# Two stages laid into one block, and the weights of two later stages prepared in the lead-in of the first

## The reference

```python
x = x + attention0(layernorm(x), c, c)   # heads of 8, softmax over 256 columns
x = x + ffn0(layernorm(x))               # of each sequence only the 32 tokens of highest score
x = x + gated_attention1(layernorm(x), c)
x = x + ffn1(layernorm(x))               # weights rounded to -1, 0, 1
x = x + softmax_attention2(layernorm(x), c)  # four square matrices Wq, Wk, Wv, Wo
x = x + gated_ffn2(x) ; ...              # and a last layer
```

## Time and profile before

| | us |
|---|---|
| runs | 1898.48, 1903.65, 1902.52 (median 1902.52) |
| profiled execution | 1898.31 (span 1896.4, mean granted TensorE clock 0.831) |
| first attention, last matmul | 450.4 |
| selected feed-forward, first matmul | 484.8 |
| block of the normed feed-forward's weights | 916.8 to 939.8 |
| block of the softmax attention's weights | 1204.8 to 1216.0 |

### The profile page before, as it was taken

The page is one execution under the profiler, slowest core; times in us unless marked ns, Lnnn a source line. Parts: engine busy times, 40 slices in busy tenths (PEclk is TensorE's granted clock), DMA queues, the critical chain, the costliest instruction groups (busy, mean ns, idle before and its releaser), DMA issues. The chain is left out here.

```text
span 1896.4 us, 32248 instructions
## 1 busy us (share of the span) xinstructions
PE 1327.3 (70%) x11572; PEld 840.8 (44%) x11572; DVE 1313.4 (69%) x2817; ACT 1104.5 (58%) x1568; POOL 577.0 (30%) x1047
## 2 busy tenths in 40 slices
PE   3999999994699758886167665489999446772111
PEld 1665566562577625554013232366666314442110
DVE  4888888882454336887679999166666467774996
ACT  2788888874121137775368888334444348874564
POOL 6566666633100041110024431101110021113663
PEclk9999999997799959997556667699999678877555
DMA  6577777663100033431200000111110300000111
GB/s 161 136 178 182 180 184 179 167 143 72 40 1 0 2 63 68 78 64 36 71 1 1 1 1 1 39 45 31 39 35 24 102 16 1 1 1 22 42 47 44
DMA packets 96676, 118.46 MB, mean 62 GB/s; under 512 B 29984, under 2 KB 82408, under 8 KB 91916
## 3 DMA queue, kind: packets, MB, share of 16 engines
q1 hardware_dynamic: 96524, 116.46, 25.0%
HBM read 80.07 MB, written 22.88 MB: 54 GB/s over the span
## 5 line engine op out<-in xcount | busy, mean ns | idle before, releaser
L592 DVE TENSOR_REDUCE ratt_nmax<-ratt_psS 128x2 f32<-128x512 f32 x512 | 318.0, 682 | 65.4 <-PE ratt_psS L420 65.0
L510 ACT ACTIVATE ratt_E<-ratt_psT 128x1024 f32<-128x1024 f32 x256 | 255.1, 1023 | 71.5 <-PE ratt_psT L438 71.3
L420 PE MATMUL ratt_psS<-ratt_K,ratt_Q 72*128 72x256 bf16 x1024 | 203.6, 283 | 22.1 <-DMA ratt_Q<-z_parts 15.9
L438 PE MATMUL ratt_psT<-ratt_Q,ratt_K 75*128 75x256 bf16 x1024 | 195.5, 274 | 0.8 <-DMA ratt_Q<-ratt_rows 0.4
L462 PE MATMUL ratt_psO<-ratt_E,ratt_V 128*32 128x256 f32 x2048 | 137.9, 387 | 0.7 <-ACT ratt_E L510 0.7
L420 PEld LDWEIGHTS ratt_psS<-ratt_K,ratt_Q 72*128 72x128 bf16 x1024 | 80.7, 99 | 112.9 <-DVE ratt_nmax L592 62.5
L438 PEld LDWEIGHTS ratt_psT<-ratt_Q,ratt_K 75*128 75x128 bf16 x1024 | 99.6, 98 | 18.0 <-issue 2.1
L3415 PE MATMUL final_psT<-final_identh,final_Z 128*128 128x128 f16 x64 | 8.3, 310 | 110.4 <-ACT final_Z L3449 110.4
L907 ACT COPY sffn_XS<-sffn_psG 128x512 f32<-128x512 f32 x8 | 4.7, 586 | 125.5 <-PE sffn_psG L856 125.5
L2217 PE MATMUL nffn_psH<-nffn_W,nffn_QT 128*128 128x512 bf16 x128 | 56.0, 588 | 28.7 <-ACT nffn_H L2296 19.9
L462 PEld LDWEIGHTS ratt_psO<-ratt_E,ratt_V 128*32 128x32 f32 x2048 | 53.6, 109 | 50.5 <-issue 27.2
(11 more groups left out here) (474 smaller groups left out, 3692.6 us busy)
## 6 DMA issues: line engine op xcount, KB each, us to landing
ratt_K<-context_parts SPq DMA_DIRECT2D x96, 192.0 KB
ratt_Q<-z_parts SPq DMA_DIRECT2D x32, 576.0 KB
gatt_V<-in_ctx_dram SPq DMA_DIRECT2D x16, 512.0 KB, 6.8
context_parts<-ratt_CS SPq DMA_DIRECT2D x48, 128.0 KB, 6.3
z_parts<-ratt_ZS SPq DMA_DIRECT2D x48, 128.0 KB, 4.6
head_sums<-ratt_O SPq DMA_DIRECT2D x64, 72.0 KB
all_X<-in_x_dram SPq DMA_DIRECT2D x16, 256.0 KB, 3.5
ratt_C<-in_ctx_dram SPq DMA_DIRECT2D x16, 256.0 KB, 3.9
```

The source lines that it names most:

```text
L420: mm = nc.tensor.matmul(psS[:, RING[h], c * D:(c + 1) * D], Q9[0:R, buf, h, n % 2, c * P:(c + 1) * P], K9[0:R, buf, h, n % 2, :], start=Tr ...
L438: mm = nc.tensor.matmul(psT[:, j % 2, e, c, :], K9[0:RM, buf, h, u, c * P:(c + 1) * P], Q9[0:RM, buf, h, u, :], start=True, stop=True)
L510: sc.activation(E[:, m % 2 * 2 + p // 2, 2 * (p % 2):2 * (p % 2) + 2], psT[:, j % 2], ACT.Exp, scale=SCALE).then_inc(exped, 1)
L592: v.tensor_reduce(nmax[:, n % 2, h, :], psS[:, RING[h]].rearrange("p (c t) -> p c t", c=2), AX.X, ALU.max, negate=True).then_inc(maxed, 1)
```

## The change

`selected_ffn` becomes a class, `SelectedFfn`, whose code is called from within the block of `first_attention`. Its tiles lie on tiles of the attention that are free by then (class `Reuse`): the weights on buffers 0 and 1 of `Q9`, its work tiles on those of `K9` and on `C`, its constants on `CS` and `ZS`, its hidden values on a part of `E`. It uses the same banks of PSUM. There is no barrier between the two any more; a group waits for the additions to `X` of its own two pairs.

The weights of `normed_ffn` and `softmax_attention` are loaded in the lead-in of the first attention into `E` and `O`, which are not in use yet, rounded and turned there, stored to DRAM (1 MB of bf16 and 1 MB of f32) and loaded in their final form at the start of their stages, whose own blocks of weights are gone. Waits on these loads stand at the start of PE's code; other engines wait for biases where they use them.

```diff
-def first_attention(nc, io, X, CT, ident, identb, zq, ck, o_dram, r_dram, ST, wsum):
+def first_attention(nc, io, X, CT, ident, identb, zq, ck, o_dram, r_dram, ST, wsum,
+                    ternaries, squares, ternary_dram, turned_dram):
+    WEIGHT_JOBS = (-4, -3, -2, -1)
...
+        ffn = SelectedFfn(
+            nc, io, s, X, ident, weights=Reuse(s, left[0]),
+            tiles=Reuse(s, left[1], C[:].rearrange("p a u m -> p (a u m)")), consts=Reuse(s, *splits),
...
             @block.sync
+                    if n == UNITS - 2:
...
+                        ffn.load_rows(sp)
+                    if n == UNITS:
+                        ffn.load_weights(sp)
+                    if n == -LEAD + 2:
+                        for m, (dram, unit) in enumerate(ternaries):
+                            sp.dma_start(wide[m].rearrange("p (c i) -> p c i", i=dram.shape[1]),
+                                         dram.rearrange("(c p) i -> p c i", p=P)).then_inc(wide_in[m], 16)
+                    if n == -LEAD + 5:
+                        for i, dram in enumerate(squares):
+                            sp.dma_start(plain[:, i], dram.rearrange("(k p) d -> p k d", p=P)).then_inc(plain_in, 16)
+                    if n == 0:
+                        sp.wait_ge(exped, job["weights", 3] + 1)
+                        sp.dma_start(ternary_dram.rearrange("p m k -> p (m k)"), ternary_out).then_inc(weights_out, 16)
+                        sp.dma_start(turned_dram.rearrange("p m k -> p (m k)"), turned_out).then_inc(weights_out, 16)
+                    if n == 1:
+                        sp.wait_ge(weights_out, 32)
...
             @block.gpsimd
+                    if n == UNITS - 1:
...
+                        ffn.constants(pool)
+                    if n == UNITS:
+                        ffn.norm.on_pool(pool, 0)
+                    if n == UNITS + 6:
+                        ffn.norm.on_pool(pool, 1)
+                with pool.Fori(2, NG) as g:
+                    ffn.norm.on_pool(pool, g)
...
             @block.tensor
+                        if p == 2 and n in WEIGHT_JOBS:
+                            i = WEIGHT_JOBS.index(n)
+                            turn_ternary(i) if i < 2 else turn_squares(i - 2)
+                        if p == 2 and n == UNITS + LAG - 1:
+                            pe.wait_ge(ffn.ready, 14)
+                            pe.wait_ge(row_out, UNITS)
+                            pe.wait_ge(maxed, UNITS * NH0)
+                            ffn.tensor_step(pe, 0, 0)
+                pe.wait_ge(exped, jobs)
+                pe.wait_ge(o_out, UNITS)
+                ffn.tensor_step(pe, 1, 1)
...
             @block.scalar
+                        if p == 2 and n in WEIGHT_JOBS:
+                            take_weights(WEIGHT_JOBS.index(n))
...
+                    if n == -LEAD + 5:
+                        for m in range(2):
+                            act.wait_ge(wide_in[m], 16)
+                            sc.activation(scratch[m], wide[m], ACT.Abs, accum_out=rowsum[:, m:m + 1]).then_inc(
+                                summed, 1)
...
             @block.vector
+                def vector_front(g, w):
+                    dve.wait_ge(added, g * 2 + 2)
+                    ffn.vector_front(dve, g, w)
+
                 for n in range(-LEAD, UNITS + 8):
+                    if n == UNITS:
...
+                        vector_front(0, 0)
+                    if n == UNITS + 4:
+                        vector_front(1, 1)
...
+                    if n == -LEAD + 6:
...
+                            step(v.tensor_scalar(wide[m], wide[m], winv[:, m:m + 1], MAGIC, ALU.mult, ALU.add))
+                            step(v.tensor_scalar(wide[m], wide[m], MAGIC, 1.0, ALU.subtract, ALU.min))
+                            v.tensor_scalar(rounded[m], wide[m], -1.0, None, ALU.max).then_inc(ternary_done, 1)
...
 def normed_ffn(...):
-        ternary(nc, "nffn_weights", identb, [(io["L1_ffn_w1"], W1, u1), (io["L1_ffn_w2"], W2, u2)],
...
+                sp.dma_start(b1[:], io["L1_ffn_b1"].rearrange("(a b) -> a b", b=P)).then_inc(b1_in, 16)
+                for tile, x in ((gam, "ln_g"), (bet, "ln_b"), (b2, "b2")):
+                    sp.dma_start(tile[:], spread(io["L1_ffn_" + x], 0, P)).then_inc(side_in, 16)
+                for m, W in enumerate((W1, W2)):
+                    sp.dma_start(W[:].rearrange("p k o -> p (k o)"), ternary_dram[:, m]).then_inc(w_in, 16)
                 sp.wait_ge(b_split, 3)
                 sp.dma_start(bias_dram.rearrange("t (a b) -> a t b", b=P), bparts[:]).then_inc(b_out, 16)
...
             def _(pe):
+                pe.wait_ge(w_in, 32)
...
 def softmax_attention(...):
-        turn_weights(nc, "satt_weights", ident,
...
+                sp.dma_start(W4[:].rearrange("p i k m -> p i (k m)"), turned_dram).then_inc(w_in, 16)
...
+                pe.wait_ge(w_in, 16)
```

More of the change, by code:

```diff
@@ L75, in spread, with pipeline, rounds @@
     return ap.unsqueeze(dim).to_broadcast(list(ap.shape[:dim]) + [n] + list(ap.shape[dim:]))
-def first_attention(nc, io, X, CT, ident, identb, zq, ck, o_dram, r_dram, ST, wsum):
+def pipeline(engine, front, back):
+    front(0, 0)
+    front(1, 1)
+    back(0, 0)
+    with engine.Fori(0, NG // 2 - 1) as h:
+        front(h * 2 + 2, 0)
+        back(h * 2 + 1, 1)
+        front(h * 2 + 3, 1)
+        back(h * 2 + 2, 0)
+    back(NG - 1, 1)
+def rounds(engine, step, last):
+    step(0, 0)
+    step(1, 1)
+    with engine.Fori(1, NG // 2 - 1) as h:
+        step(h * 2, 0)
+        step(h * 2 + 1, 1)
+    for g in range(NG - 2, last + 1):
+        step(g, g % 2)
```

610 lines of the change are left out of this document (353 added, 257 removed).

## The result

The changed kernel takes 1838.08 us, the median of 4 runs (1836.06 to 1840.84), against 1901.41 beside it: a ratio of 0.9669, 95% interval 0.965 to 0.9688. The forecast was 1840 in 1824 to 1864. The profiled execution took 1840.84 (span 1839.1), 57.5 less than that of before.

A forecast was written before the change was run, and what follows sets the result against it. No single engine was taken to bound the kernel; the bound changes by stage, with PE idle between stages. Terms -36 - 19.5 - 9.5 + 5 = -60 gave 1838.3 from the profiled execution or 1842.5 from the median; forecast 1840, range 1824 to 1864.

The forecast's parts named there:

- join: Seam between first attention and selected feed-forward: without the barrier group 1 widens earlier, less a charge for the tail; -36 us.
- normed feed-forward: Start of that stage: its 23.0 us weights' block goes, 0.4 and 3.1 charged for the split bias's delay; -19.5 us.
- softmax attention: Start of that stage: 11.2 us block goes, PE's first matmul waits 1.6 to 3.5 longer, lower end taken; -9.5 us.
- lead-in: Start of first attention: the added weight preparation delays unit 0 by 1 + 0.9 + 3; +5 us.
- the 2 us for group 1's norm: At the seam: group 1's scores come 2 us later, as POOL's part of the norm stands behind a pair's addition.
- the 2.6 for group 2's scores: At the seam: 2.6 us charged because POOL does group 2's norm only behind the late last addition to X.
- the step for POOL and DVE: Lead-in: DVE's rounding holds up POOL, +3 us; by the skill's exclusive lock POOL loses 7.5, making the lead-in +9.5.
- The other two steps of the lead-in: Lead-in: loads ahead of stores and pair 1's inputs cost 1 us; ACT's sums ahead of C's first parts cost 0.9.
- The rival of the smaller gain at the seam: Seam: weights land at 458, not 453.5, and POOL's norm of group 2 is 10 late; only -22, 1854 us; chance 0.16.
- The dear lead-in: Lead-in costs 16 us: rounding locks POOL out and stores hold up the first units' rows; 1851 us; chance 0.13.
- The other side: Selected feed-forward stays at the low clock: +154, 1994 us; chance 0.04 together with anything else that loses.
- no overlap: Seam: group 0's preparation is held until the last addition to X, saving only some 5 us; 1871 us; chance 0.04.

The follow-up runs named there:

- e6: Changed kernel with the selected feed-forward's 2 MB of weights issued ahead of the store of pair 14's sums, not behind it: 1835.81 us.
- e7: Changed kernel, normed feed-forward's three rows loaded behind the split bias, softmax attention's matrices loaded first with PE's wait moved to the first projection: 1832.86 us.
- e9: The changed kernel run once more, unaltered, as a yardstick: 1839.62 us.
- e3: Changed kernel with the lead-in's rounding on DVE cut to one operation for each matrix instead of three, giving other weights: 1837.64 us.
- e5: Changed kernel with ACT's two sums of magnitudes one step later, behind its first part of C of pair 1: 1836.53 us.
- e12: Changed kernel with the edits of e4, e5, e6 and e7 together: 1826.23 us, ratio 0.9613 to the kernel before.
- e4: Changed kernel with PE turning the four square matrices ahead of the two rounded ones in the lead-in: 1838.89 us.
- e10: Changed kernel with e12's edits plus two added matmuls after each score of units 0 to 2, to keep PE busy: 1839.95 us.

## Why the prediction was right

| term | forecast | measured in the changed kernel |
|---|---|---|
| join (last product to group 1's widening) | -36 | 28.76 - 65.74 = -37.0 |
| normed feed-forward (last addition to first weights) | -19.5 | 15.75 - 34.83 = -19.1 |
| softmax attention (last addition to first projection) | -9.5 | 10.14 - 19.91 = -9.8 |
| lead-in | +5 | +3.9 at the first scores, +7.0 at the attention's end |
| sum | -60 | -58.9 (profiled executions: -57.5; 1.4 are in none of the terms) |

- The join was right in mechanism and, in part by luck, in size. The weights were forecast to wait PE about 3 us after the last product; the widening came 6.5 after it, for 3.16 of which PE waited for them, as they took up to 11.5 us to land and not the 9 that were allowed. Against that, the 2 us for group 1's norm and the 2.6 for group 2's scores were not felt: L330 to L330 is 22.2 us, as before, and L305 does not wait. The two errors hang together: the late weights gave group 1's scores the time they needed. e6 takes the lateness away, and a wait of 2.87 us for these scores comes up. "The mask is there when the last matmul ends" was not quite so: PE waited 1.15 for DVE's picks.
- For the normed feed-forward the forecast named the right wait: the split bias comes back late, behind 2.2 MB. e7 takes 1.1 MB of it away and gains 3.7, where 3.1 was charged for all of it.
- For the softmax attention the lower end was the right one to take; PE waited 1.3 us longer after the stage's start (6.5 against 5.2).
- In the lead-in the step for POOL and DVE held: 3 us forecast, 2.8 measured at three operations. By the rows, POOL's three operations and DVE's three take 2.91 and 3.75 us by themselves, 6.66 together, and 6.4 passed from 19.93 to 26.33: they took turns, each of them stretched, and neither stood throughout. The Trainium skill (SBUF — State Buffer, "Who interferes with whom") has the two engines share one pair of ports as an exclusive lock. That the operations took turns agrees with it; the 7.5 us of loss for POOL that the prediction worked out by it did not come, and neither did +9.5 for the lead-in at the first scores, since the second matrix's rounding met only one operation of POOL's that ran long (L697, 2.24) and then a POOL that stood.
- The other two steps of the lead-in were both a little small: 1.4 for ACT's sums where 0.9 was charged, and about 1.3 for the stores behind the loads where 1 was. "The queues are under half busy after 6 us" disagrees with the prediction's own row, a DMA share of 0.58 from 16 to 26 us. K's delay came to 5.3; only 3.9 of it reached the first scores, where PE's own chain ended at about the same time.
- The term had no place for what comes behind the first scores: 3.1 us more up to the attention's end, of which about 1.7 go with the longer stretch at the lower clock and 1.4 with the wait for the rows of maxima, which e9 does not have. So the +5 lies between the two measured numbers in part by luck.
- The rival of the smaller gain at the seam came near in its condition and not in its price: the weights were there 6.5 us after the last product, as late as its 458 would be, but L305 of group 2 did not wait. The dear lead-in fell, with +7.0 where 16 was its price. The other side fell too: the feed-forward's clock is 0.99 from 463.9 on. So did "no overlap": PE is idle at the seam for 4.3 of 6.5 us.
- Of the signs, group 1's widening at 28.8 us (25 to 27 were named) and the normed feed-forward's first weights at 15.75 (13 to 15) lie just outside; the others came.

## What to carry to other kernels

A load taken out of a gap pays by what the gap was waiting for, so look for the second-latest arrival before pricing it: at the normed feed-forward the returning bias and the queue in front of it, not the weights; at the seam the scores of group 1, which showed as soon as the load came early. Work moved into an idle-looking lead-in lengthens whatever chain passes there. Where two chains end together, as K and Q from DRAM and PE's turnings here, an edit of one alone hardly moves what both lead to; read a later place as well before calling it worth nothing, as e3 to e5 gained 2.5 to 3.4 at the attention's end and e12, which moves both chains, 4.9. Filling an engine with spare work to hold its clock is a gamble on the clock's state when it begins: at the attention's end it gave 3.3 us in one order and cost 12 in another.

## What the runs showed of the hardware

The kernel before ran its first units at half rate, though its windows read a granted clock of 1.00. Two of its rows, a pair of turned scores before and after 56 us, and the window of the first:

```profile
48.25 0.63 PE L438 MATMUL ratt_psT<-ratt_Q,ratt_K 75*128 75x256 bf16 x2
...
56.99 0.39 PE L438 MATMUL ratt_psT<-ratt_Q,ratt_K 75*128 75x256 bf16 x2
```

```profile
48.00:56.00 8.00, 8.00 (x46) 5.24 (x47) 6.51 (x11) 4.21 (x5) 4.77 (x12) 1.00 0.30 85
```

So in these executions, ahead of the first recorded change of level, 1.00 stands for either level: half rate in the kernel before, the high rate in the changed kernel's first scores. A matmul's duration tells which. In the changed kernel the first scores ran at the high rate (0.82 us for 6, where 12 took 3.17 before), straight behind the turnings; in e4, where PE stood for 3.11 us between the two, at the low one (5 in 1.22). And a busy PE did not bring the clock back in e10: it was at 1.2 GHz from 33 to 73 us with PE busy for 40.00 of these 40 us, and rose only with the turned scores under way. What brings it back is not settled here.
